# Graph attention and three message-passing layers on one core: the padded last edge group left out, the last loop body outside the loop

## The chip, the cores and the metric

The kernel runs on one core of one Trainium2 chip. The metric is the device time in microseconds (us) of a whole launch, smaller is better. A core has five engines with a program each: TensorE (PE in the profile; PEld is its weight load), VectorE (DVE), ScalarE (ACT), GpSimd (POOL) and SyncE (SP), and they meet only at semaphores.

## What is computed

A graph has 6250 nodes with 128 features and E = 200000 edges, sorted by their target `dst`. Four stages go over all edges: one attention layer (4 heads, softmax over the edges of each target), and three gated message-passing layers. Between them are dense steps over the nodes.

```python
def _L0_gnn_ref(x, edge_index, W, att):
    xh = (x @ W).reshape(-1, H, C)
    xi = xh[dst]
    xj = xh[src]
    alpha = (xi * a_i).sum(-1) + (xj * a_j).sum(-1)
    alpha = jax.nn.leaky_relu(alpha, SLOPE)
    amax = jax.ops.segment_max(alpha, dst, num_segments=N)
    ex = jnp.exp(alpha - amax[dst])
    denom = jax.ops.segment_sum(ex, dst, num_segments=N)
    alpha = ex / (denom[dst] + 1e-16)
    out = jax.ops.segment_sum(xj * alpha[..., None], dst, num_segments=N)
...
for l in range(L):                       # L = 3
    h = emb                              # for l > 0: normalised over the nodes
    e = jnp.concatenate([h[dst], h[src]], axis=1)
    hk = jax.nn.relu(e @ linA_w[l].T + linA_b[l])
    w = jax.nn.sigmoid(hk @ linB_w[l].T + linB_b[l])
    prop = jax.ops.segment_sum(w * h[src], dst, num_segments=N)
    emb = jax.nn.relu(jnp.concatenate([h, prop], axis=1) @ lin_w[l].T + lin_b[l])
...
x = _layernorm(x + _L0_gnn_ref(x, edge_index, L0_gnn_W, L0_gnn_att), axis=-1)
x = _layernorm(x + _L1_gnn_ref(x, edge_index, ...), axis=-1)
```

## The kernel before

**Groups.** Edges are worked off in groups of GE = 512 (128 partitions x 4 columns; edge 4p + t of a group stands in partition p, column t). The lists of edges are laid out in QP = 98 rows of CQ = 4 groups, so NG = QP * CQ = 392 groups are run (lines 103 to 105). 200000 edges are 390 full groups and 320 edges: group 390 (the 391st) is 5/8 full, and group 391 (the 392nd) holds no edge at all. Both lists are filled with padding first (lines 932 and 933): `dstI` with 16 * N, which matches no node, and `srcI` with 0. A padded place therefore gathers row 0 of the table like any other place would gather its own row, and its contribution is zero. In group 390 the padded places are columns 0 to 3 of partitions 80 to 127, 48 of the 128 rows of each of its four gathers; in group 391 they are all 128 of each.

**An edge stage.** GpSimd's program (from line 653) gathers the source rows: `gather` (from line 665) waits until the group's slot in the ring `G` of U = 8 slots is free (line 668, not in the first turn) and until ScalarE has copied the group's indices (line 669), and issues four indirect DMAs of 128 rows of 1 KB (line 672), whose ends count up `gathered[u]`. SyncE fetches, per four groups, the targets' offsets inside a window of 32 nodes, and per group the window's rows. Then, in the message-passing stages:

- VectorE `mp_selT` (line 1411) makes a selection matrix, TensorE `mp_hk` (line 1717) spreads the window's target terms with it, VectorE `mp_hidden` (line 1426) adds the gathered source terms: it is the first to need the gather. `mp_logit` (line 1437) does the relu and the dot product, ScalarE `gate_of` (line 876) the sigmoid, VectorE `mp_C` (line 1446) the weighted selection, TensorE `mp_agg` (line 1727) the sum over edges, VectorE `mp_E` (line 1457) adds it to the accumulator.
- In the attention stage TensorE `gat_sjT` (line 1587) is the first to need the gather; the chain goes on over `gat_e8` (lines 1599, 1603), `gat_den` (1614), `gat_nd` (1622, 1625) and VectorE's small steps up to `gat_acc` (line 1217).

Each stage is a software pipeline written out by hand: `step(k0, off)` runs, for group k0 + off, the parts of this group and of groups some steps behind (the lags in `gat_order` and `mp_order`), in this order for VectorE in a message-passing stage:

```python
mp_order = ((1, mp_hidden), (4, mp_E), (0, mp_selT), (1, mp_logit), (2, mp_C), (0, mp_sel))
```

**The loop.** On every engine a stage is: the first turn of 8 groups written out (groups 0 to 7), a hardware loop `Fori(1, NG // U)` of 48 turns of 8 groups (groups 8 to 391), and a drain, `step(NG, off, new=False)`, which only finishes the lagging parts. VectorE reads the windows' bases from memory into registers at the start of each turn (`load_bases`, line 1048, 16 registers in a turn of the loop). Behind an edge stage everything waits for the accumulator: `gat["acc"]` reaches NG before the first layer norm, `mp["acc"]` reaches km + NG before ScalarE's `hT` (line 903), from which the next layer's table, and so its first gather, is made. For groups whose edges reach beyond one window there is a further block, `extra_windows`; with these inputs its body is not run in the profile.

Of the kernel before, what the change touches and what calls it, by code (L numbers as in the profile page):

```python
# [20 lines left out]
P = 128  # L21
T = 4
GE = P * T
# [68 lines left out]
def gnn_kernel(nc, x, src, dst, W0, att, linA_w, linA_b, linB_w, linB_b, lin_w, lin_b, gamma, beta, final_w, final_b,  # L92
# [12 lines left out]
    NG = QP * CQ  # L105
    assert NG % U == 0 and QP <= P and L * 4 * D + D <= U * T * 2 * D - NBLK * D
# [33 lines left out]
    with ExitStack() as ctx:  # L140
# [73 lines left out]
        def room(lo, width):  # L214
# [106 lines left out]
        gat = dict(ahead=True, rows=lambda k, off: (gathered[off % U], 8 * k + 64 * (off // U + 1)),  # L321
                              window=lambda k, off: (win_in[off % 4], 4 * k + 16 * (off // 4 + 1)),
                              offsets=lambda k, off: (offs_in[off // 4 % 2], 2 * k + 16 * (off // U + 1)), **gat_sems)
        mp = dict(ahead=True, rows=lambda k, off: (gathered[off % U], 8 * k + (8 * NG + 64 * (off // U + 1))),
                             window=lambda k, off: (win_in[off % 4], 4 * k + (4 * NG + 16 * (off // 4 + 1))),
                             offsets=lambda k, off: (offs_in[off // 4 % 2], 2 * k + (2 * NG + 16 * (off // U + 1))),
                             **mp_sems)
# [11 lines left out]
        def one_by_one(sems, w):  # L339

            return dict(ahead=False, rows=lambda k, off: (x_rows, w * 64 + 64),
                                   window=lambda k, off: (x_win, w * 32 + 32),
                                   offsets=lambda k, off: (x_win, w * 32 + 32), **sems)
# [133 lines left out]
        def _(sp):  # L477
# [82 lines left out]
            def gat_body(k0):  # L560
                starts = load_starts(k0)
                for off in range(U):
# [5 lines left out]
            with sp.Fori(1, NG // U) as turn:  # L568
                gat_body(turn * U)
            with extra_windows(sp, 0) as at:  # L570
# [18 lines left out]
            sp.wait_ge(gat["acc"], NG)  # L589
# [3 lines left out]
            for l in range(L):  # L593
                kl = l * NG
# [28 lines left out]
                def body(k0):  # L623
                    starts = load_starts(k0)
                    for off in range(U):
# [5 lines left out]
                with sp.Fori(1, NG // U) as turn:  # L631
                    body(turn * U)
                with extra_windows(sp, l + 1) as at:
# [20 lines left out]
        def _(pool):  # L654
# [34 lines left out]
            with pool.Fori(1, NG // U) as turn:  # L689
                k0 = turn * U  # L690
                for off in range(U):
                    gather(T0, TW, k0, off, k0, (gat["R"], k0 + (off - U + 1)))
            with extra_windows(pool, 0) as at:
# [11 lines left out]
            for l in range(L):  # L705
                kl = l * NG
# [4 lines left out]
                with pool.Fori(1, NG // U) as turn:  # L711
# [8 lines left out]
        def _(act):  # L720
# [66 lines left out]
            def gat_step(k0, off, new=True):  # L787
                if new:
                    if reached(k0, off, U - LOOKAHEAD):
                        idx_slot_past(k0, off, 8 * k0)  # L790
                    copy_idx(k0, off + LOOKAHEAD)
                    gat_pen(k0, off)
                if reached(k0, off, 2) and (new or off < 2):
                    gat_exp(k0, off - 2)
                if reached(k0, off, 3):
# [4 lines left out]
            with act.Fori(1, NG // U) as turn:  # L800
# [3 lines left out]
            for off in range(3):  # L804
                gat_step(NG, off, new=False)
# [5 lines left out]
            with extra_windows(act, 0) as at:  # L811
                copy_idx_extra(at)
                for stage in (gat_pen, gat_exp, gat_den4):
                    stage(NG + at.n, 0, one_by_one(gat_sems, at.w))
# [23 lines left out]
            act.wait_ge(gat["acc"], NG)  # L838
            node_steps(act, NT // 2, ((0, ln_block), (7, ln_sqrt), (10, ln_to_x1), (10, ln_to_h)), BL)

            for l in range(L):
                kl = l * NG
                km = kl + windows_before(act, l)

                def idx_ahead(k0, off):
                    idx_slot_past(k0, off, 8 * kl + 8 * k0 + 8 * NG)
                    copy_idx(k0, off + LOOKAHEAD)

                for off in range(U - LOOKAHEAD):
                    idx_ahead(0, off)  # L850
# [28 lines left out]
                def step(k0, off, new=True):  # L879
                    if reached(k0, off, U - LOOKAHEAD) and new:  # L880
                        idx_ahead(k0, off)
                    if reached(k0, off, 1):
# [4 lines left out]
                with act.Fori(1, NG // U) as turn:  # L887
# [3 lines left out]
                step(NG, 0, new=False)  # L891

                with extra_windows(act, l + 1) as at:
                    copy_idx_extra(at)
                    gate_of(NG + at.n, 0, one_by_one(mp_sems, at.w))


                act.wait_ge(mp["acc"], km + NG)
# [31 lines left out]
        def _(dve):  # L930
# [133 lines left out]
            def gat_selT(k0, off, done=gat):  # L1064
# [3 lines left out]
                dve.wait_ge(*done["offsets"](k0, off))  # L1068
# [20 lines left out]
            def gat_mxs(k0, off, done=gat):  # L1089
                m, w = mx[:, off % 4, :], off % 4  # L1090
                dve.wait_ge(*done["window"](k0, off))
# [133 lines left out]
            def gat_step(k0, off, new=True):  # L1225
                for lag, stage in gat_order:
                    if reached(k0, off, lag) and (new or off < lag):
# [8 lines left out]
            with dve.Fori(1, NG // U) as turn:  # L1236
# [4 lines left out]
            load_bases(NG, -U, 0)  # L1241
            for off in range(5):
                gat_step(NG, off, new=False)
# [17 lines left out]
            dve.wait_ge(gat["acc"], NG)  # L1261
# [22 lines left out]
            with extra_windows(dve, 0) as at:  # L1284
                now, k0 = one_by_one(gat_sems, at.w), NG + at.n
                dve.wait_ge(x_free, at.w + (at.q + 1))
                base[0] = at.node
                make_extra_sel(at, selT16, P, pF[:, 1:2], now["selT"], now["sel"], now["window"](0, 0))
# [66 lines left out]
            for l in range(L):  # L1355
                kl = l * NG
# [50 lines left out]
                def mp_selT(k0, off, done=mp):  # L1407
                    if reached(k0, off, 4, done):
                        dve.wait_ge(done["hk"], km + k0 + (off - 3))
                    dve.wait_ge(*done["offsets"](kl + k0, off))  # L1410
# [10 lines left out]
                def mp_hidden(k0, off, done=mp):  # L1421
                    dve.wait_ge(*done["rows"](kl + k0, off))
# [38 lines left out]
                def step(k0, off, new=True):  # L1461
                    for lag, stage in mp_order:
                        if reached(k0, off, lag) and (new or off < lag):
# [7 lines left out]
                with dve.Fori(1, NG // U) as turn:  # L1471
# [4 lines left out]
                load_bases(NG, -U, 0)  # L1476
                for off in range(4):
                    step(NG, off, new=False)

                dve.wait_ge(mp["acc"], km + NG)  # L1480
                dve.sem_inc(x_free, 1)
                with extra_windows(dve, l + 1) as at:
                    now, k0 = one_by_one(mp_sems, at.w), NG + at.n
                    dve.wait_ge(x_free, at.w + (at.q + 1))
                    base[0] = at.node
                    make_extra_sel(at, selT16, S * W, pF[0:S * W, 5:6], now["selT"], now["sel"], now["window"](0, 0))
# [53 lines left out]
        def _(pe):  # L1540
# [40 lines left out]
            def gat_sjT(k0, off, done=gat):  # L1581
# [3 lines left out]
                pe.wait_ge(*done["rows"](k0, off))  # L1585
# [43 lines left out]
            def gat_step(k0, off, new=True):  # L1629
                if new:  # L1630
                    gat_sjT(k0, off)
                for lag, stage in ((3, gat_den), (4, gat_nd), (1, gat_e8)):
                    if reached(k0, off, lag) and (new or off < lag):
# [4 lines left out]
            with pe.Fori(1, NG // U) as turn:  # L1638
# [3 lines left out]
            for off in range(4):  # L1642
# [147 lines left out]
```

## Time and profile before

| | |
|---|---|
| time of the runs, median of 3 | 8248.64 us (8248.41 to 8270.31) |
| the profiled execution's own time | 8252.02 us |
| its span in the profile | 8250.5 us |
| POOL busy | 5982.9 us (73%) |
| DVE busy | 4942.3 us (60%) |
| PE busy | 4840.5 us (59%) |
| ACT busy | 1354.9 us (16%) |
| indirect DMAs issued by POOL | 6272 (1568 per stage) |
| granted TensorE clock, mean | 0.514 |

How to read it: the span runs from the first to the last instruction of the profiled execution; the 1.5 us between it and that execution's time are start and end around it. "Issue" in a chain or behind a wait is time in which the engine waited for nothing that the profile shows. A DMA's entry in the chain runs from its issue to its landing. An engine's idle time costs something only where the end of a stage waits for it.

### The profile page before, as it was taken

The numbers are of one execution on the slowest core, as the hardware profiler recorded it, in microseconds if no ns is written. First come the engines' busy times: TensorE is split into PE (matmuls) and PEld (weight loads), VectorE is DVE, ScalarE is ACT, GpSimd is POOL, SyncE is SP. The second block draws the span as 40 slices with busy tenths as digits, with TensorE's granted clock in tenths as the row PEclk, the third lists the DMA queues.
The fourth block names the chain that finished last, engine by engine and source line by source line (L and its number), as shares of the span: only waits on it lengthen the run. The fifth ranks groups of instructions, "written<-read, shape, count | busy, mean of one in ns | idle before, by whom it ended". The sixth has DMA issues, their size and how long they took to land.

```text
span 8250.5 us, 135185 instructions
## 1 busy us (share of the span) xinstructions
PE 4840.5 (59%) x26722; PEld 4122.7 (50%) x26723; DVE 4942.3 (60%) x26175; ACT 1354.9 (16%) x5278; POOL 5982.9 (73%) x6332
## 2 busy tenths in 40 slices
PE   5888888888744544454464444444546444544555
PEld 4777777777644444444444444444445444444444
DVE  7777777778755555555555555555555555555555
ACT  2333333333400000000020000000011000000002
POOL 4777777777477777777757777777766777777775
PEclk6555555555655555555565555555556555555555
DMA  4444444444444444444454444444445444444443
GB/s 135 131 131 133 131 131 131 133 132 131 127 129 131 129 129 129 130 129 130 129 152 130 129 129 131 129 129 131 129 115 166 129 130 130 129 130 130 129 129 102
DMA packets 615022, 1076.11 MB, mean 130 GB/s; under 512 B 307424, under 2 KB 372864, under 8 KB 614436
## 3 DMA queue, kind: packets, MB, share of 16 engines
q0 software_dynamic: 301056, 822.48, 35.6%
q1 hardware_dynamic: 307316, 247.87, 10.1%
q10 hardware_dynamic: 6356, 3.20, 0.2%
q14 instruction: 276, 2.26, 0.1%
q8 instruction: 18, 0.29, 0.0%
HBM read 1027.54 MB, written 45.47 MB: 130 GB/s over the span
## 4 chain that ended last, share of the span: by engine, by line
POOL 46%; issue 22%; PE 12%; DMA 9%; DVE 8%; DVEq 2%; POOLq 1%; ACT 1%; SPq 0%; ACTq 0%
POOL G L672 46%; DMA G<-mp_rows,idx 5%; DMA G<-gat_rows,idx 4%; PE ps L1727 3%; PE ps L1625 3%; DVE junk L1437 2%; PE ps L1587 2%; PE ps L1622 1%; PE ps L1614 1%; DVEq L1048 1%; PE ps L1679 0%; PE ps L1680 0%; DVE weighted L1196 0%; DVE selw L1446 0%; POOLq L669 0%
## 5 line engine op out<-in xcount | busy, mean ns | idle before, releaser
L672 POOL DMA_INDIRECT G<-mp_rows,idx x4704 | 4450.6, 946 | 1571.6 <-issue 1374.0
L1727 PE MATMUL ps<-selw,G 128*128 128x32 f32 x9408 | 2222.3, 400 | 595.8 <-DVE selw L1446 595.2
L1727 PEld LDWEIGHTS ps<-selw,G 128*128 128x128 f32 x9408 | 2094.0, 328 | 878.2 <-issue 759.3
L1426 DVE TENSOR_TENSOR pen<-ps,G 128x512 f32<-128x512 f32 x1176 | 812.9, 691 | 2740.2 <-DMA G<-mp_rows,idx 2736.3
L1717 PE MATMUL ps<-awin,ring 96*128 96x128 bf16 x4704 | 715.0, 307 | 2326.5 <-DVE ring L1411 2324.0
L672 POOL DMA_INDIRECT G<-gat_rows,idx x1568 | 1492.6, 952 | 519.8 <-issue 483.8
L1717 PEld LDWEIGHTS ps<-awin,ring 96*128 96x128 bf16 x4704 | 411.8, 132 | 2476.1 <-DVE ring L1411 2473.3
L876 ACT ACTIVATE gate<-logit,params 128x4 f32<-128x4 f32 x1176 | 349.5, 297 | 5340.9 <-DVE junk L1437 5291.5
L1437 DVE SCALAR_TENSOR_TENSOR junk<-pen,ps 128x128 f32<-128x128 f32 x4704 | 1060.4, 278 | 0.1
L1411 DVE TENSOR_TENSOR ring<-ring,ps 96x512 bf16<-96x512 bf16 x1176 | 795.6, 676 | 38.5 <-DMA ring<-rel_dst 38.5
L1625 PE MATMUL ps<-sel,weighted 128*128 128x32 f32 x3136 | 750.8, 404 | 0.0
L1625 PEld LDWEIGHTS ps<-sel,weighted 128*128 128x128 f32 x3136 | 698.0, 327 | 25.3
L1587 PE MATMUL ps<-ident,G 128*128 128x128 f32 x1568 | 428.5, 429 | 228.3 <-DMA G<-gat_rows,idx 225.8
L762 ACT ACTIVATE pen<-ring,negbig 128x512 f32<-128x512 bf16 x392 | 282.8, 722 | 1182.2 <-DVE ring L1060 1179.9
L1587 PEld LDWEIGHTS ps<-ident,G 128*128 128x128 f32 x1568 | 280.7, 217 | 251.2 <-issue 121.1
L1086 DVE CUSTOM_DVE_ANT_0 junk<-ps,pen 128x512 f32<-128x512 f32 x392 | 267.4, 682 | 217.8 <-issue 149.7
L1437 DVE DVE_READ_ACCUMULATOR junk<-pen,ps 128x1 f32 x4704 | 370.4, 79 | 0.0
L1416 DVE TENSOR_TENSOR ps<-ps,rel_all 128x128 f32<-128x128 f32 x1176 | 335.2, 285 | 0.0
L1446 DVE TENSOR_TENSOR selw<-ps,gate 128x128 f32<-128x128 f32 x1176 | 331.7, 282 | 0.2
L1614 PE MATMUL ps<-sel,ex 128*4 128x32 f32 x3136 | 231.0, 238 | 122.4 <-DVE tt L1211 122.4
L750 ACT COPY idx<-idx_all 128x4 int32 (+1 forms) x1572 | 284.0, 181 | 31.0 <-issue 24.8
L1614 PEld LDWEIGHTS ps<-sel,ex 128*4 128x4 f32 x3136 | 162.1, 105 | 253.4 <-issue 201.1
(200 smaller groups left out, 4748.8 us busy)
## 6 DMA issues: line engine op xcount, KB each, us to landing
ring<-rel_dst SPq DMA_DIRECT2D x294, 384.0 KB
G<-mp_rows,idx POOLq DMA_INDIRECT x4704
ring<-rel_dst SPq DMA_DIRECT2D x98, 512.0 KB
awin<-mp_dst_rows SPq DMA_DIRECT2D x1176, 24.0 KB
G<-gat_rows,idx POOLq DMA_INDIRECT x1568
mp_rows<-acc SPq DMA_DIRECT2D x36, 512.0 KB, 3.0
mp_dst_rows<-acc SPq DMA_DIRECT2D x36, 384.0 KB, 5.4
gat_rows<-ring SPq DMA_DIRECT2D x50, 128.0 KB, 1.9
```

The lines of the kernel that those rows point to most:

```text
L672: pool.indirect_dma_start(out=G[:, u, width * t:width * (t + 1)], out_offset=None, in_=table, in_offset=bass.IndirectOffsetOnAxis(ap=idx[: ...
L876: nc.scalar.activation(gate[:, off % 4, :], logit[:, off % 4, :], ACT.Sigmoid, bias=params[:, l, C_BB:C_BB + 1]).then_inc(done["gate"], 1)
L1411: v.tensor_tensor(selT16[0:S * W, off % 4, :], relbc16[0:S * W, off % U, :], nodeP[0:S * W, :].to_broadcast([S * W, GE]), ALU.is_equal).th ...
L1416: v.tensor_tensor(selP[:, off % 4, :].rearrange("p (t n) -> p t n", t=T), iotaP.unsqueeze(1).to_broadcast([P, T, W]), rel4, ALU.is_equal). ...
L1426: v.tensor_tensor(pen[:, off % 2, :].rearrange("p (t c) -> p t c", t=T), PS[off % 2][:, :].rearrange("p (t c) -> p t c", t=T), Grows[:, of ...
L1437: v.scalar_tensor_tensor(junk[:, P * t:P * t + P], pen[:, off % 2, P * t:P * t + P], 0.0, wP, ALU.max, ALU.mult, accum_out=logit[:, off % ...
L1446: v.tensor_tensor(selw[:, off % 4, :].rearrange("p (t n) -> p t n", t=T), one.rearrange("p (t n) -> p t n", t=T), gate[:, off % 4, :].unsq ...
L1587: i = tr(PS[off % 2][:, P * t:P * t + P], Grows[:, off % U, t, D:2 * D], ident[:, :])
L1614: i = mm(PS[4 + b][0:H, 2 * W:3 * W], ex4[:, b, H * t:H * t + H], sel[:, off % U, W * t:W * t + W], start=(t == 0), stop=(t == T - 1))
L1625: i = mm(PS[4 + b][:, 0:W], R[:, b, D * t:D * t + D], sel[:, off % U, W * t:W * t + W], start=(t == 0), stop=(t == T - 1))
L1717: i = mm(PS[off % 2][:, D * t:D * t + D], selT16[0:S * W, off % 4, P * t:P * t + P], awin[:, off % 4, :], start=True, stop=True)
L1727: i = mm(PS[2 + off % 2][:, 0:W], Grows[:, off % U, t, 0:D], selw[:, off % 4, W * t:W * t + W], start=(t == 0), stop=(t == T - 1))
```

## The change

Every stage runs GR = 391 groups. The loop runs 47 turns (groups 8 to 383) instead of 48; the last body, now with groups 384 to 390, is written out behind it together with the drain (`step(LAST, off, REST)`, LAST = 384, REST = 7). A part of a step is left out where its group would be 391. Waits that counted to 392 per stage count to 391, and those that count the landings of a ring slot take into account that slot 7 (and window slot 3) lands once less per stage. ScalarE's copies of indices, which run four groups ahead, skip group 391 but still make the first four of the next stage. The change core; the same replacement of the loop's bounds stands on all five engines:

```diff
     NG = QP * CQ
+    GR = -(-E // GE)
+    LAST = NG - U
+    REST = GR - LAST
+    assert REST == U - 1
...
+        def rows_landed(stage, k0, off):
+
+            whole = 64 * (NG // U - (off % U == U - 1))
+            return gathered[off % U], 8 * k0 + (stage * whole + 64 * (off // U + 1))
...
-                kl = l * NG
+                kl = l * GR
                 km = kl + windows_before(pool, l)
                 pool.wait_ge(t1_out, 16 * NQ * (l + 1))
                 for off in range(U):
-                    gather(T1, TW, 0, off, kl + NG, None)
-                with pool.Fori(1, NG // U) as turn:
+                    gather(T1, TW, 0, off, kl + GR, None)
+                with pool.Fori(1, NG // U - 1) as turn:
                     k0 = turn * U
                     for off in range(U):
-                        gather(T1, TW, k0, off, kl + k0 + NG, (mp["agg"], km + k0 + (off - U + 1)))
+                        gather(T1, TW, k0, off, kl + k0 + GR, (mp["agg"], km + k0 + (off - U + 1)))
+                for off in range(REST):
+                    gather(T1, TW, LAST, off, kl + (LAST + GR), (mp["agg"], km + (LAST + off - U + 1)))
...
-            def idx_slot_past(k0, off, before):
-
-                act.wait_ge(gathered[(off + LOOKAHEAD) % U], before + 64 * ((off + LOOKAHEAD) // U))
...
+            def idx_ahead(stage, k0, off, stop):
+
+                if off < U and (off + LOOKAHEAD < stop or off + LOOKAHEAD >= U):
+                    if stage > 0 or reached(k0, off, U - LOOKAHEAD):
+                        act.wait_ge(*rows_landed(stage, k0, off + LOOKAHEAD - U))
                     copy_idx(k0, off + LOOKAHEAD)
...
-                def step(k0, off, new=True):
+                def step(k0, off, stop=U):
                     for lag, stage in mp_order:
-                        if reached(k0, off, lag) and (new or off < lag):
+                        if reached(k0, off, lag) and off - lag < stop:
                             stage(k0, off - lag)
...
-                with dve.Fori(1, NG // U) as turn:
+                with dve.Fori(1, NG // U - 1) as turn:
                     k0 = turn * U
                     load_bases(k0, -U, U)
                     for off in range(U):
                         step(k0, off)
-                load_bases(NG, -U, 0)
-                for off in range(4):
-                    step(NG, off, new=False)
-
-                dve.wait_ge(mp["acc"], km + NG)
+                load_bases(LAST, -U, U)
+                for off in range(REST + 4):
+                    step(LAST, off, REST)
+
+                dve.wait_ge(mp["acc"], km + GR)
```

What stands on GpSimd in the first message-passing stage, before: the loop's last group, its end, and then at once the loads of the block of further windows (line 452).

```order
114 L672 DMA G<-mp_rows,idx 128x256 x4
115 L669 REGISTER_ALU
116 L672 DMA G<-mp_rows,idx 128x256 x4
117 L711 REGISTER_ALU
118 L711 COMPARE_AND_BRANCH
119 L452 TENSOR_LOAD windows
```

And in the change, the same place; of the seven groups of four gathers behind the loop's branch the first and the last two stand here.

```order
117 L687 DMA G<-mp_rows,idx 128x256 x4
118 L728 REGISTER_ALU
119 L728 COMPARE_AND_BRANCH
120 L683 REGISTER_ALU
121 L687 DMA G<-mp_rows,idx 128x256 x4
```

```order
130 L683 REGISTER_ALU
131 L687 DMA G<-mp_rows,idx 128x256 x4
132 L683 REGISTER_ALU
133 L687 DMA G<-mp_rows,idx 128x256 x4
134 L465 TENSOR_LOAD windows
```

The program is 28 gathers longer there, and everything behind it in GpSimd's program stands at another place in memory than before; up to the first stage's loop nothing on any engine has moved but the numbers in the instructions.

VectorE's end of the same stage in the change: the last step with a new group, then the drain.

```order
1337 L1433 TENSOR_TENSOR ps<-ps,rel_all 128x128
1338 L1442 REGISTER_ALU
1339 L1443 TENSOR_TENSOR pen<-ps,G 128x512
1340 L1474 ISA
1341 L1474 TENSOR_TENSOR acc<-acc,ps 128x32
1342 L1454 SCALAR_TENSOR_TENSOR junk,logit<-pen,ps 128x128 x4
1343 L1463 TENSOR_TENSOR selw<-ps,gate 128x128
1344 L1474 ISA
1345 L1474 TENSOR_TENSOR acc<-acc,ps 128x32
1346 L1463 TENSOR_TENSOR selw<-ps,gate 128x128
1347 L1474 ISA
1348 L1474 TENSOR_TENSOR acc<-acc,ps 128x32
```

The hidden layer's step (`mp_hidden`, line 1443 in the change, 1426 before) at number 1339 is that of group 390; behind it stands what stood behind group 391's before, without a `mp_selT` between.

## Rows read from the trace of the kernel before

**Rows 1.** The page: busy time, and the chain that ended last by engine and line.

```profile
PE 4840.5 (59%) x26722; PEld 4122.7 (50%) x26723; DVE 4942.3 (60%) x26175; ACT 1354.9 (16%) x5278; POOL 5982.9 (73%) x6332
...
POOL 46%; issue 22%; PE 12%; DMA 9%; DVE 8%; DVEq 2%; POOLq 1%; ACT 1%; SPq 0%; ACTq 0%
```

**Rows 2.** Timeline: start, duration, engine, line, instruction, idle before; first message-passing stage, POOL.

```profile
2195.81 0.96 POOL L672 DMA_INDIRECT G<-mp_rows,idx  x1 [34.75 <-DMA mp_rows<-acc]
...
4150.56 0.95 POOL L672 DMA_INDIRECT G<-mp_rows,idx  x1 [0.30 <-issue]
4151.81 0.95 POOL L672 DMA_INDIRECT G<-mp_rows,idx  x1 [0.30 <-issue]
...
4155.56 0.95 POOL L672 DMA_INDIRECT G<-mp_rows,idx  x1 [0.30 <-issue]
```

**Rows 3.** Timeline, all engines, end of the first message-passing stage (groups 389, 390, 391).

```profile
4148.39 0.69 DVE L1426 TENSOR_TENSOR pen<-ps,G 128x512 f32<-128x512 f32 x1 [2.38 <-DMA G<-mp_rows,idx]
...
4153.50 0.69 DVE L1426 TENSOR_TENSOR pen<-ps,G 128x512 f32<-128x512 f32 x1 [2.49 <-DMA G<-mp_rows,idx]
...
4160.61 0.69 DVE L1426 TENSOR_TENSOR pen<-ps,G 128x512 f32<-128x512 f32 x1 [4.49 <-DMA G<-mp_rows,idx]
...
4162.61 3.62 PE L1727 MATMUL ps<-selw,G 128*128 128x32 f32 x16 [4.73 <-DVE selw L1446]
...
4166.37 0.19 DVE L1457 TENSOR_TENSOR acc<-acc,ps 128x32 f32 x1 [1.52 <-PE ps L1727]
```

**Rows 4.** Busy time by stretch, same place: last columns PEclk, DMA share, GB/s.

```profile
4145.00:4150.00 5.00, 2.49 (x14) 2.12 (x13) 2.62 (x14) 0.38 (x2) 3.78 (x5) 0.50 0.36 102
...
4157.50:4160.00 2.50, 0.39 (x2) 0.25 (x2) 0.00 (x0) 0.00 (x0) 0.00 (x0) 0.50 0.80 72
4160.00:4162.50 2.50, 0.00 (x0) 0.00 (x0) 1.85 (x12) 0.11 (x1) 0.00 (x0) 0.50 0.00 0
```

**Rows 5.** Timeline, VectorE, ends of the second and the third message-passing stage.

```profile
6165.89 0.69 DVE L1426 TENSOR_TENSOR pen<-ps,G 128x512 f32<-128x512 f32 x1 [2.42 <-DMA G<-mp_rows,idx]
...
6173.12 0.69 DVE L1426 TENSOR_TENSOR pen<-ps,G 128x512 f32<-128x512 f32 x1 [4.61 <-DMA G<-mp_rows,idx]
...
8180.28 0.69 DVE L1426 TENSOR_TENSOR pen<-ps,G 128x512 f32<-128x512 f32 x1 [2.45 <-DMA G<-mp_rows,idx]
...
8188.22 0.69 DVE L1426 TENSOR_TENSOR pen<-ps,G 128x512 f32<-128x512 f32 x1 [5.32 <-DMA G<-mp_rows,idx]
```

**Rows 6.** The chain in order of time, third message-passing stage: start, us, what.

```profile
8182.33 5.29 DMA G<-mp_rows,idx
...
8187.73 0.04 DVEq L1425
8187.77 0.45 issue
```

**Rows 7.** Timeline, TensorE, end of the attention stage (groups 388, 390, 391).

```profile
2061.67 1.09 PE L1587 MATMUL ps<-ident,G 128*128 128x128 f32 x4 [0.54 <-DMA G<-gat_rows,idx]
...
2071.82 1.09 PE L1587 MATMUL ps<-ident,G 128*128 128x128 f32 x4 [0.95 <-DMA G<-gat_rows,idx]
2078.57 1.09 PE L1587 MATMUL ps<-ident,G 128*128 128x128 f32 x4 [2.55 <-DMA G<-gat_rows,idx]
```

**Rows 8.** Who waited for whom, 2230 to 4155 us: total us, times, longest us.

```profile
POOL G L672 <- issue: 442.0, 1451, 0.3
POOL G L672 <- PE ps L1727: 15.5, 51, 0.3
```

**Rows 9.** The chain, attention stage: VectorE at the start of a turn.

```profile
1999.15 2.34 issue
2001.61 1.11 DVEq L1048
```

**Rows 10.** Timeline, VectorE, start of the last turn of the attention stage's loop.

```profile
2043.66 0.69 DVE L1086 CUSTOM_DVE_ANT_0 junk<-ps,pen 128x512 f32<-128x512 f32 x1 [4.21 <-issue]
```

**Rows 11.** Timeline, VectorE, the final layer norm's loop of ten blocks a turn.

```profile
8226.42 0.16 DVE L1532 SCALAR_TENSOR_TENSOR bnm<-bmv,brs 128x1 f32<-128x1 f32 x1 [0.24 <-issue]
...
8235.34 0.16 DVE L1532 SCALAR_TENSOR_TENSOR bnm<-bmv,brs 128x1 f32<-128x1 f32 x1 [0.24 <-issue]
```

More of the change, by code:

```diff
@@ L567, in _ @@
             gat_body(0)
-            with sp.Fori(1, NG // U) as turn:
+            with sp.Fori(1, NG // U - 1) as turn:
                 gat_body(turn * U)
+            gat_body(LAST, REST)
             with extra_windows(sp, 0) as at:
@@ L799, in _ @@
                 gat_step(0, off)
-            with act.Fori(1, NG // U) as turn:
+            with act.Fori(1, NG // U - 1) as turn:
                 k0 = turn * U
@@ L803, in _ @@
                     gat_step(k0, off)
-            for off in range(3):
-                gat_step(NG, off, new=False)
+            for off in range(REST + 3):
+                gat_step(LAST, off, REST)
             def copy_idx_extra(at):
@@ L886, in _ @@
                     step(0, off)
-                with act.Fori(1, NG // U) as turn:
+                with act.Fori(1, NG // U - 1) as turn:
                     k0 = turn * U
@@ L890, in _ @@
                         step(k0, off)
[L891 removed]
+                for off in range(REST + 1):
+                    step(LAST, off, REST)
                 with extra_windows(act, l + 1) as at:
                     copy_idx_extra(at)
[L895 to L898 removed]
+                    gate_of(GR + at.n, 0, one_by_one(mp_sems, at.w))
+                act.wait_ge(mp["acc"], km + GR)
                 act.sem_inc(waited, 1)
@@ L1240, in _ @@
                     gat_step(k0, off)
-            load_bases(NG, -U, 0)
-            for off in range(5):
-                gat_step(NG, off, new=False)
+            load_bases(LAST, -U, U)
+            for off in range(REST + 5):
+                gat_step(LAST, off, REST)
             def make_extra_sel(at, tile, rows, node, selT_done, sel_done, window):
@@ L1470, in _ @@
                     step(0, off)
-                with dve.Fori(1, NG // U) as turn:
+                with dve.Fori(1, NG // U - 1) as turn:
                     k0 = turn * U
@@ L1627, in gat_nd, with gat_step @@
                 i.then_inc(done["nd"], 1)
[L1629 to L1633, printed above, removed]
+            def gat_step(k0, off, stop=U):
+                for lag, stage in ((0, gat_sjT), (3, gat_den), (4, gat_nd), (1, gat_e8)):
+                    if reached(k0, off, lag) and off - lag < stop:
                         stage(k0, off - lag)
@@ L1637, in _ @@
                 gat_step(0, off)
-            with pe.Fori(1, NG // U) as turn:
+            with pe.Fori(1, NG // U - 1) as turn:
                 k0 = turn * U
@@ L1641, in _ @@
                     gat_step(k0, off)
-            for off in range(4):
-                gat_step(NG, off, new=False)
+            for off in range(REST + 4):
+                gat_step(LAST, off, REST)
             with extra_windows(pe, 0) as at:
                 for stage in (gat_sjT, gat_e8, gat_den, gat_nd):
-                    stage(NG + at.n, 0, one_by_one(gat_sems, at.w))
+                    stage(GR + at.n, 0, one_by_one(gat_sems, at.w))
             def ln_turn(turn, off):
@@ L1738, in _ @@
                     step(0, off)
-                with pe.Fori(1, NG // U) as turn:
+                with pe.Fori(1, NG // U - 1) as turn:
                     k0 = turn * U
@@ L1742, in _ @@
                         step(k0, off)
-                for off in range(3):
-                    step(NG, off, new=False)
+                for off in range(REST + 3):
+                    step(LAST, off, REST)
                 with extra_windows(pe, l + 1) as at:
                     for stage in (mp_hk, mp_agg):
-                        stage(NG + at.n, 0, one_by_one(mp_sems, at.w))
+                        stage(GR + at.n, 0, one_by_one(mp_sems, at.w))
             def f_linear(turn, off):
```

108 lines of the change are left out of this document (54 added, 54 removed).

## Prediction

> **What bounds the kernel now.** I read the page first, then GpSimd's timeline inside a stage and at its end, then all engines at the four stage ends. No engine is full: GpSimd is busy 73% of the span, yet the chain that ended last is GpSimd and its "issue" to 68% [rows 1]. The timeline tells why: a gather takes 0.95 us and the next one starts 0.30 us later, always, so 1.25 us apart. From the first gather of the first message-passing stage at 2195.81 to its 1568th at 4155.56 are 1567 steps of 1.2506 us [rows 2]. What GpSimd has to issue sets the time inside a stage: four gathers, 5.00 us a group. The other engines wait in each group (VectorE 2.38 us before group 389's hidden layer, [rows 3]).
>
> At the end of a stage another thing counts. The last gather of group 390 is issued at 4150.56 [rows 2] and the step that needs it starts at 4153.50 [rows 3], 2.94 us later. The last of group 391 is issued at 4155.56 and its step starts at 4160.61, 5.05 us later: this landing is 2.11 us late. Group 391 is all padding, its 512 places all gather row 0. While they are under way the DMA engines are 0.80 busy and move 72 GB/s, where they were 0.36 busy at 102 GB/s before, and after the landing they are idle [rows 4]: 0.80/72 against 0.36/102 is 3.1 times the DMA time per byte. A gather is 128 KB (131072 bytes), which at 72 GB/s is 1.8 us, longer than the 1.25 us between issues, so the four queue up: 4 x 1.8 = 7.3 us from about 4153 ends at 4160.4. So I read the late landing as the price of 128 reads of one address, that is, of the padding, and not of standing last.
>
> **The change, part by part.**
>
> *One group less, message-passing stages.* The chain goes gather, hidden layer, logit, gate, weighted selection, sum, accumulator, and then the relu for all nodes. Behind the hidden layer of the stage's last group the drain has the same instructions before and after, in the same order (the last excerpt of the order shows it), and the engines are idle when it starts. So the end moves by the distance between the starts of the last two hidden layers: 4160.61 - 4153.50 = 7.11 us in the first stage [rows 3]; 6173.12 - 6165.89 = 7.23 and 8188.22 - 8180.28 = 7.94 in the other two [rows 5]. In each 5.00 are the four gathers not issued, and the rest is lateness. The third has more because its landing took 5.29 us and VectorE then spent 0.45 us on "issue" between wait and work [rows 6], against 4.85 us, and nothing of the kind, in the first.
>
> *The attention stage.* Here TensorE's transposes need the gather first: 2078.57 for group 391, 2071.82 for group 390 [rows 7], 6.75 us apart. The drain behind is again the same; it is longer, but it is a chain of its own length and starts 6.75 us earlier.
>
> *Sum of the gains:* 7.11 + 7.23 + 7.94 + 6.75 = 29.0 us.
>
> *Leaving the loop earlier.* All engines leave the loop seven groups before the end and go on in straight code; a loop was left once per stage before too, but GpSimd had nothing to issue behind it. Only a pause on GpSimd would count in full. From below it is nothing: GpSimd's gaps stay at 0.3 us at the longest, over the whole loop with its 48 branches back [rows 8], and the first turn is straight code of the same kind. From above take the longest pause of the sort in the trace, VectorE's 2.34 us of "issue" at the start of a turn of the attention loop [rows 9], four times 9.4 us. I take the lower end, being GpSimd's own rows, with 0.1 us a stage for unevenness: 0.5 us, rounded up. The Trainium skill (Runtime: NRT & Kernel Launch, "Instruction fetch mechanics") says that instructions are fetched ahead in blocks strictly in sequence, and that only a taken branch out of the two blocks held stalls. Leaving a loop takes no branch, so by that rule the term is 0 and the gain 29.0. By the upper end of the rows the gain would be 19.6.
>
> *The other engines' exits.* VectorE needs 2.34 us and then 1.11 us for the register load at a turn's start [rows 9]. In the attention stage it stands 4.21 us before group 384's step [rows 10], yet at group 388 TensorE waits for the gather again (0.54 us, [rows 7]): caught up in four groups. The new tail has seven. In the message-passing stages a group leaves 2.4 us free [rows 3], so such a pause is gone a group or two later. Cost 0, hidden under GpSimd's issues; if that cover were gone, up to 4.2 us in one stage.
>
> *Padding that stays.* Group 390 has 48 padded rows of 128 in each gather. Its landing (2.94 us) is 0.11 us behind that of group 389 (4148.39 - 4145.56 = 2.83, the issue being four steps of 1.25 before the 4150.56 of [rows 2]). This is in the distances above already. *Registers, waits with other counts, the index copies four groups ahead:* the same number of instructions for each group that is left, and ScalarE is 16% busy [rows 1]: 0.
>
> Net: 29.0 - 0.5 = 28.5 us. The profiled execution took 8252.0 us (its span 8250.5 and 1.5 around it), so the sum gives 8223.5 for such a one; the median of the runs shown is 3.4 lower, 8248.6, and from there it gives 8220.1. I predict **8220**.
>
> **The rivals.**
>
> *B, the last gather lands late whatever it reads.* Then group 390's last landing would take 5 us too, and only the four issues are saved: 4 x 5.00 = 20.0 us, 8228.6. For it: all the late ones seen stand last. Against it: the DMA engines were busy at a low rate [rows 4], not idle.
>
> *C, GpSimd pauses where it leaves the loop*, 2.34 us at most in each stage [rows 9]: gain 19.1 to 28.5 us, 8220 to 8229.5. For it: VectorE has such pauses. Against: GpSimd has none [rows 8].
>
> *D, slower: the moved loops.* GpSimd's program grows by 28 gathers per stage, so the three message-passing loops stand elsewhere in memory. If a loop there fits the fetch less well, each of its turns pauses: 3 x 47 = 141 turns. At 28.5/141 = 0.20 us a turn the gain is gone, at (28.5 + 24.7)/141 = 0.38 us the kernel is measurably slower. The final layer norm's loop on VectorE shows 0.24 us once per turn, 8.9 us apart [rows 11]: that price gives 34 us, and 8254; 2.34 us a turn would give 8550. Against it: GpSimd's loop of the first message-passing stage, already at another place than the attention stage's, shows no pause at all [rows 8]. The same section of the Trainium skill (Runtime: NRT & Kernel Launch, "Instruction fetch mechanics") speaks for this case: a branch back to a block no longer held stalls. By that rule it would decide whether GpSimd's loop spans more than two blocks, which no run here shows.
>
> *That the change doesn't drop the group* is ruled out by the order of instructions: 28 gathers stand behind the loop, not 32.
>
> **How the numbers follow.** About 0.3% (24.7 us) is what a measurement of this kernel can tell from no change. My forecast 0.67, B 0.12, C 0.16, D 0.05. The forecast lies only 3.8 us beyond that bound, and the runs before spread over 22 us, so 0.07 of its 0.67 may come out as no change; B falls wholly in there, C nearly so (0.02 beyond), and D for 0.02, with 0.03 slower. Faster 0.62, same 0.35, slower 0.03. The range: if every stage gained the third's 7.94 us the sum would be 31.8 and the time 8217, less a little, 8216; at the other end B and C end at 8229, and a median like the profiled execution is 3.4 higher: 8233.
>
> **What would show it.** Right: 1564 gathers per stage, 1.25 us apart through the loop's end; the last hidden layer of each message-passing stage about 2.9 us behind the last issue, with 4.6 to 5.3 us of VectorE's idle time before it gone to 2.5; no stretch with the DMA engines at 0.8 and 72 GB/s; each stage 6.7 to 7.9 us shorter, nothing changed between the stages. Wrong: a last landing of 5 us (B); a gap over 0.3 us on GpSimd 28 gathers before a stage's end (C), or once per 32 gathers in the loop (D).

## The result, and the profile after

The changed kernel took 8217.6 us (median of 7 runs, 8216.4 to 8238.9), the kernel before on the same chip 8248.1 (7 runs, 8246.5 to 8270.3): 30.5 us less, ratio 0.9965 with a 95% interval of 0.9956 to 0.9975, which is a gain of 21 to 36 us. Predicted were 8220 us and a gain of 28.5.

The profiled execution of the change is its slowest: 8238.9 us (span 8237.1), the first of its seven; the first of before was 22 us above its median too. So its rows carry about 21 us that the median does not have, and the first rows show where they lie. The page, busy time, the chain and GpSimd's two groups:

```profile
PE 4828.4 (59%) x26657; PEld 4110.2 (50%) x26658; DVE 4929.9 (60%) x26111; ACT 1352.1 (16%) x5266; POOL 5983.1 (73%) x6316
...
POOL 46%; issue 22%; PE 11%; DMA 9%; DVE 8%; DVEq 2%; POOLq 1%; ACT 1%; SPq 0%; ACTq 0%
...
L687 POOL DMA_INDIRECT G<-mp_rows,idx x4692 | 4450.8, 949 | 1564.2 <-issue 1383.9
...
L687 POOL DMA_INDIRECT G<-gat_rows,idx x1564 | 1492.4, 954 | 519.5 <-issue 483.5
```

Against [rows 1] there are 16 gathers fewer, and GpSimd is busy for the same time: one takes 949 ns where the execution before had 946. The timeline of GpSimd over the first message-passing stage shows it as a spacing, the counterpart of [rows 2]:

```profile
2192.37 0.97 POOL L687 DMA_INDIRECT G<-mp_rows,idx  x1 [34.08 <-DMA mp_rows<-acc]
...
4116.68 0.95 POOL L687 DMA_INDIRECT G<-mp_rows,idx  x1 [0.30 <-issue]
4117.94 0.95 POOL L687 DMA_INDIRECT G<-mp_rows,idx  x1 [0.30 <-issue]
...
4151.80 0.95 POOL L687 DMA_INDIRECT G<-mp_rows,idx  x1 [0.30 <-issue]
4202.91 0.95 POOL L687 DMA_INDIRECT G<-mp_rows,idx  x1 [50.16 <-DMA mp_rows<-acc]
```

1563 steps between 2192.37 and 4151.80 are 1.2536 us each, against 1.2506 before. Over the four stages the wider spacing comes to 16.5 us (20.0 - 3.47 of the table below), most of the excess of this execution. Twenty-eight gathers before the end, at 4116.68 to 4117.94, GpSimd leaves the loop, and the gap is the usual 0.30 us. In all four stages of the change no gap between two gathers is above 0.32 us.

The end of the same stage, all engines, then VectorE in the second and third stage and TensorE in the attention stage, against [rows 3, 5, 7]:

```profile
4149.65 0.69 DVE L1443 TENSOR_TENSOR pen<-ps,G 128x512 f32<-128x512 f32 x1 [2.44 <-DMA G<-mp_rows,idx]
...
4154.86 0.69 DVE L1443 TENSOR_TENSOR pen<-ps,G 128x512 f32<-128x512 f32 x1 [2.59 <-DMA G<-mp_rows,idx]
...
4160.69 0.19 DVE L1474 TENSOR_TENSOR acc<-acc,ps 128x32 f32 x1 [1.52 <-PE ps L1742]
...
6164.87 0.69 DVE L1443 TENSOR_TENSOR pen<-ps,G 128x512 f32<-128x512 f32 x1 [2.58 <-DMA G<-mp_rows,idx]
...
8175.25 0.69 DVE L1443 TENSOR_TENSOR pen<-ps,G 128x512 f32<-128x512 f32 x1 [2.50 <-DMA G<-mp_rows,idx]
...
2076.12 1.09 PE L1604 MATMUL ps<-ident,G 128*128 128x128 f32 x4 [0.90 <-DMA G<-gat_rows,idx]
```

VectorE's idle time before a stage's last hidden layer was 4.49, 4.61 and 5.32 us and is 2.59, 2.58 and 2.50. The last step starts 3.06 us behind the last issue (4154.86 against 4151.80), where it was 5.05. Busy time by stretch, against [rows 4] (last columns DMA share and GB/s):

```profile
4149.00:4154.00 5.00, 2.44 (x13) 2.13 (x12) 2.62 (x13) 0.38 (x2) 2.85 (x3) 0.50 0.35 103
4154.00:4156.50 2.50, 0.10 (x1) 0.00 (x0) 1.60 (x9) 0.00 (x0) 0.00 (x0) 0.50 0.02 7
```

The stretch with the DMA engines at 0.80 and 72 GB/s is gone; they keep their usual share (0.35 at 103 GB/s) nearly to the last landing.

The span closes to the hundredth when it is cut at the gathers. T is a stage's time from its first to its last gather, D the time from there to the next stage's first gather, in the last row to the end of the span.

| us | T before | T after | D before | D after |
|---|---|---|---|---|
| attention | 1968.96 | 1967.85 | 122.05 | 119.26 |
| message passing 1 | 1959.75 | 1959.43 | 52.46 | 51.11 |
| message passing 2 | 1959.94 | 1958.92 | 54.14 | 51.31 |
| message passing 3 | 1960.23 | 1959.21 | 68.17 | 64.75 |

With the first gather 0.46 us later (105.26 against 104.80) that is 3.47 + 10.39 - 0.46 = 13.4 us, as the two spans say. The 3.47 are 4 x 5.0 us not issued, less what the wider spacing gave back in this execution; the 10.39 stand at the stages' ends. With before's spacing the sum is 20.0 + 10.4 - 0.5 = 29.9, beside the 30.5 of the medians.

### The profile page after: what moved, and what is told of

Its sections match the earlier page's. It is cut to its first block, busy times and chain, and to the rows that moved or that the text cites. A ratio compares the mean times of both kernels' runs of the same rounds, so it can differ in the third digit from the quotient of the medians.

```text
span 8237.1 us, 134783 instructions
## 1 busy us (share of the span) xinstructions
PE 4828.4 (59%) x26657; PEld 4110.2 (50%) x26658; DVE 4929.9 (60%) x26111; ACT 1352.1 (16%) x5266; POOL 5983.1 (73%) x6316
## 4 chain that ended last, share of the span: by engine, by line
POOL 46%; issue 22%; PE 11%; DMA 9%; DVE 8%; DVEq 2%; POOLq 1%; ACT 1%; SPq 0%; ACTq 0%
POOL G L687 46%; DMA G<-mp_rows,idx 5%; PE ps L1742 3%; DMA G<-gat_rows,idx 3%; PE ps L1642 3%; DVE junk L1454 2%; PE ps L1604 1%; PE ps L1639 1%; PE ps L1631 1%; DVEq L1065 1%; PE ps L1694 0%; PE ps L1695 0%; DVE selw L1463 0%; DVE sel L1073 0%; POOLq L684 0%
```

## The experiments

The theory (A): the padded group is late because each of its gathers reads one row 128 times. The main rival (B): it is late because it is last. Also open was what the peeling costs by itself.

The runs came on four chips, and these differ. On three of them the kernel before took 10448 to 10453 us, on the fourth 8249 us, as in the first measurement. Each result stands beside runs of before on its own chip.

### Padding spread, and the change taken apart

The first edit, on the kernel before, fills the 704 padded places (192 in group 390, 512 in group 391; the third series' expectation says 576, which is wrong) with real row numbers:

```diff
+            sp.dma_start(srcI[QF:QF + 1, E - QF * QW:QW],
+                         src[0:QW - (E - QF * QW)].rearrange("(q e) -> q e", q=1)).then_inc(edges_loaded, 16)
...
-            dve.wait_ge(edges_loaded, 96)
+            dve.wait_ge(edges_loaded, 112)
```

> The kernel before, all 392 groups and loops, but the 704 padded places of src hold the sources of the first 704 edges instead of 0, so that group 391 reads 512 different rows. Theory A (the last landing is late because 128 descriptors read one row): group 391's step starts about 2.9 us behind its last issue, as group 389's did, and the four lateness terms go, 2.11 + 2.23 + 2.94 + 1.75 = 9.0 us: 8239 us against 8248. Rival B (the last gather is late whatever it reads): no change, 8248 us, and 5 us from last issue to step.

The second is the change with the same edit.

> The changed kernel with the padded places of group 390 spread over different rows in the same way. Theory A: group 390's landing was only 0.1 us late, so at most 0.5 us over four stages, not to be told from the change. Rival B: the same, 0. A gain of over 3 us would mean that 48 padded rows of 128 cost more at a stage's end than I read.

The third is the change with eight groups in the last body, 392 in all, so that of the change only the peeling is left, with its rewritten waits and index copies:

```diff
-    GR = -(-E // GE)
+    GR = NG
...
-            whole = 64 * (NG // U - (off % U == U - 1))
+            whole = 64 * (NG // U)
...
-            whole = 16 * (NG // 4 - (off % 4 == 3))
+            whole = 16 * (NG // 4)
```

> The changed kernel's code, but with 392 groups: the loop runs 47 turns and the last eight groups stand outside. The code moved as in the change, nothing is left out. My sum (pauses at the loop's exit 0.5 us in all, moved loops 0): 8248 to 8249 us, and GpSimd's gaps 0.30 us at 32 gathers before a stage's end. Rival C (a pause of up to 2.34 us per stage on GpSimd): up to 8257. Rival D (moved loops pause each turn): 8282 or more.

The fourth is the first with group 203, far from any end, reading row 0 only:

```diff
+            then(v.memset(idx_all[:, 203 * T:204 * T], 0))
```

> The padding spread as in the first, and the indices of group 203 (in the middle of each stage) all set to 0, so that its gathers read one row: this group's sources are wrong for the output. Theory A: group 203's step starts about 2 us late, 5 us behind its last issue, with the DMA engines near 0.8 busy at some 72 GB/s, and group 204 about on time or little late; the stage's end isn't later, since GpSimd goes on at 1.25 us, and no late landing at its end. Rival B: nothing late in the middle, and group 391's landing 5 us.

These four ran on a chip where before takes 10452.7 us. A second series has the change itself in place of the second kernel, and its chip was of the same sort:

> The kernel before with its padded places reading different rows, once more, since the first four kernels ran on a chip where the kernel before took 10453 us and GpSimd waited for landings inside the stages: there a stage's end says little. Where the kernel before takes 8248: theory A 8239 us (ratio 0.9989) and the last landing of each stage 2.9 us behind its issue; rival B 8248 us and 5 us. Where it takes 10450 again, neither shows in the time, as before.

> The change itself beside the others on one chip. At 8248 for the kernel before: 8217 to 8221 us, as first measured. On a chip like the last, where the stages are bound by landings of 5.4 to 7.6 us a group: 391 of 392 groups, a gain of 5.4 x 3 + 7.6 = 24 us or a little more, about 10428 of 10452.

> 392 groups, 47 turns and eight groups outside the loop. On the last chip this read 1.0013 (1.0004 to 1.0022), 13 us slower, where the runs of the kernel before spread over 32 us. At 8248 for the kernel before: my theory 8248 to 8249 us, rival C up to 8257, rival D 8282 or more. If the 13 us come again, the code's new place costs something that the first comparison of the change hid.

> Padding spread, and group 203's indices all 0, so that group reads one row in the middle of each stage (its sources are wrong for the output). Theory A: step of group 203 about 5 us behind its last issue, neighbours 2.9 us, the DMA engines near 0.8 busy at 72 GB/s for some 2 us, the last landing of the stage 2.9 us. Rival B: group 203 as its neighbours, last landing 5 us.

| | median us | before us | ratio (95%) |
|---|---|---|---|
| spread, first series | 10447.0 | 10452.7 | 0.9998 (0.9989 to 1.0007) |
| change and spread | 10435.5 | 10452.7 | 0.9990 (0.9981 to 0.9999) |
| peeling alone, first series | 10465.7 | 10452.7 | 1.0013 (1.0004 to 1.0022) |
| group 203, first series | 10450.4 | 10452.7 | one run |
| spread, second series | 10451.1 | 10450.5 | 1.0002 (0.9992 to 1.0011) |
| the change itself | 10434.4 | 10450.5 | 0.9984 (0.9975 to 0.9993) |
| peeling alone, second series | 10460.4 | 10450.5 | 1.0011 (1.0002 to 1.0020) |
| group 203, second series | 10457.0 | 10450.5 | one run |

What these chips do differently the profile of the spread kernel shows (second series). First its page, then VectorE in the middle of the first message-passing stage, then two stretches there:

```profile
another core or an unknown queue 45%; DVE 24%; issue 17%; PE 10%; DVEq 4%; ACT 0%; DMA 0%; SPq 0%; POOL 0%; ACTq 0%; POOLq 0%
...
L1428 DVE TENSOR_TENSOR pen<-ps,G 128x512 f32<-128x512 f32 x1176 | 806.7, 686 | 3860.3 <-remote 3709.2
```

```profile
4006.48 0.69 DVE L1428 TENSOR_TENSOR pen<-ps,G 128x512 f32<-128x512 f32 x1 [8.67 <-remote]
...
4009.01 0.68 DVE L1428 TENSOR_TENSOR pen<-ps,G 128x512 f32<-128x512 f32 x1
...
4011.53 0.68 DVE L1428 TENSOR_TENSOR pen<-ps,G 128x512 f32<-128x512 f32 x1
...
4024.89 0.69 DVE L1428 TENSOR_TENSOR pen<-ps,G 128x512 f32<-128x512 f32 x1 [10.75 <-remote]
```

```profile
4002.50:4005.00 2.50, 0.00 (x0) 0.00 (x0) 0.00 (x0) 0.00 (x0) 1.35 (x2) 0.50 0.35 103
4005.00:4007.50 2.50, 0.00 (x0) 0.00 (x0) 1.02 (x3) 0.00 (x0) 0.26 (x1) 0.50 0.10 36
```

GpSimd's issues no longer head the chain. VectorE waits (8.67 and 10.75 us here) for something the profile has no name for, ahead of the step that needs the gather, then works off groups 2.52 us apart. In the wait the DMA engines fall to 0.10, so bandwidth is not what is short. Nor do the gathers keep the engines longer: the page gives their queue 27.5% of 10452.7 us, 0.46 us a gather, against 35.6% of 8250.5 us and 0.47 us before. A message-passing group takes 2336.8 us / 391.75 = 5.96 us here (T of the first such stage) instead of 5.00, an attention group 3015.8 / 391.75 = 7.70. What holds the landings back no run here tells.

What follows from the two series. *Padding, by the clock: undecided.* At the end of the first message-passing stage of the spread kernel (second series) VectorE still has five groups to work off: their hidden layers start 2.70 to 12.81 us behind the last issue, 2.52 us apart. Behind such a backlog a last landing that is 2 us late moves nothing, so A and B forecast the same, and neither the spread padding nor group 203 moved the time. *Peeling alone costs* 13.0 and 9.8 us by the medians. *The group left out gains* what one group takes in each stage: from peeling alone to the change, on one chip, 10460.4 - 10434.4 = 26.0 us, beside 3 x 5.96 + 7.70 = 25.6. The whole change is 16.1 us faster there, and its interval still excludes 1. The change with spread padding, 17.2 us faster by the medians on another chip, is not to be told from the change: spreading the 48 padded rows left in each gather of group 390 shows no gain here.

*Padding, by the trace: one row is slow to read there too.* The first message-passing stage's end, peeling alone (padding as in before) and then the spread kernel, second series:

```profile
5585.00:5587.50 2.50, 0.61 (x4) 0.34 (x4) 2.33 (x12) 0.09 (x1) 0.12 (x1) 0.50 0.83 80
```

```profile
5587.50:5590.00 2.50, 1.98 (x11) 1.75 (x9) 0.87 (x8) 0.38 (x2) 0.95 (x1) 0.50 0.38 105
5590.00:5592.50 2.50, 0.81 (x5) 0.41 (x5) 2.30 (x12) 0.05 (x1) 0.00 (x0) 0.50 0.04 10
```

With the same group at the same place, the last gathers ran at 0.83 and 80 GB/s when they read one row and at 0.38 and 105 GB/s when they read many. And in the middle of a stage, behind the one-row gathers of group 203, which GpSimd issued at 6865.01 to 6868.76 in the second message-passing stage (first series):

```profile
6862.50:6865.00 2.50, 0.06 (x1) 0.06 (x1) 0.00 (x0) 0.49 (x2) 1.89 (x2) 0.50 0.36 105
...
6867.50:6870.00 2.50, 0.00 (x0) 0.00 (x0) 0.00 (x0) 0.00 (x0) 1.89 (x2) 0.50 0.70 89
6870.00:6872.50 2.50, 0.00 (x0) 0.00 (x0) 0.41 (x1) 0.00 (x0) 0.00 (x0) 0.50 0.72 77
```

In the second series a stretch behind group 203's gathers has 0.66 at 77 GB/s in the same stage. The high share goes with the row, not with the end. That speaks against B, but in a share, not yet in microseconds; how late group 203's own step was can't be read under VectorE's backlog.

### Every gather from one row, or from the same 128 rows

To get the price into the time whatever the chip, it was made large in two more kernels. The first is before with this, ahead of the first gather:

```diff
+            then(v.memset(idx_all[:, :], 0))
```

> The kernel before with the whole table of gather indices set to 0, so all 6272 gathers read row 0 128 times, as the padded group's do; the sums over edges are therefore of row 0 alone, all else runs as before. Theory A (descriptors that read one and the same row cost the DMA engines about three times as much per byte, and that is why the padded group lands late): the DMA engines' share rises from about 0.36 at 102 GB/s to 0.75 or more at 70 to 90 GB/s all through the edge stages. At the 0.80 and 72 GB/s of rows 4, a gather of 128 KB fills the engines for 1.46 us, more than the 1.25 us in which GpSimd issues one: on the chip of the first profile the time would be 9000 us or more, on the slower chip of the last runs at least what it is. Rival B (the last group is late because it is the last, whatever it reads): share 0.36, and the time of before within 0.3%.

The second repeats column 0 of the index table in all columns:

```diff
+            then(v.tensor_copy(idx_all[:, 1:], idx_all[:, 0:1].to_broadcast([P, (NG + LOOKAHEAD) * T - 1])))
```

> The kernel before with every column of the table of gather indices set to column 0, so all 6272 gathers read the same 128 scattered rows, one each per partition; the sums over edges are of those rows alone, all else runs as before. Theory A (it is one and the same row within a gather that costs): share about 0.36 at about 102 GB/s wherever GpSimd is not waiting, and the time of before within 0.3%. Rival C (it is a small stretch of memory read over and over, not one row, that costs): share clearly above 0.36 at the same GB/s, and the time between that of before and that of the run with one row.

This chip was like the first: before took 8249.4 us. One row: **11629.5 us**. The same 128 rows: **8249.8 us**. (One run each; the first is off by 3380 us, for the second the rows below count, not the clock.) The stretch from 4000 to 5000 us for one row, from 3000 to 4000 for the same 128 rows and for before:

```profile
4000.00:5000.00 1000.00, 352.16 (x1693) 299.58 (x1692) 369.45 (x1836) 55.55 (x282) 532.93 (x564) 0.50 1.00 91
```

```profile
3000.00:4000.00 1000.00, 498.40 (x2399) 424.44 (x2398) 523.88 (x2600) 78.66 (x399) 756.37 (x800) 0.50 0.45 129
```

```profile
3000.00:4000.00 1000.00, 498.87 (x2400) 424.86 (x2400) 524.00 (x2600) 78.89 (x400) 756.29 (x801) 0.50 0.46 130
```

With one row the DMA engines are full, and 564 gathers take 1000 us: one every 1.77 us. The other transfers have their share in that. The gathers' own queue stands on the two pages, one row first, then before:

```profile
q0 software_dynamic: 301056, 822.48, 86.4%
```

```profile
q0 software_dynamic: 301056, 822.48, 35.6%
```

86.4% of 11627.9 us over 6272 gathers is 1.60 us of all the engines for each, against 0.47 us: 3.4 times as much for the same bytes. Reading the same 128 rows 6272 times costs nothing. So it is the same row within a gather that costs, not a small set of rows read over and over (rival C of that expectation falls, for scattered rows; 128 neighbouring rows were not tried).

The second kernel also decides A against B on the fast sort of chip, since its padded group reads 128 rows like all others, and it leaves the loops as before does. VectorE and GpSimd at the end of the first message-passing stage:

```profile
4159.80 0.94 POOL L672 DMA_INDIRECT G<-mp_rows,idx  x1 [0.30 <-issue]
4210.13 0.94 POOL L672 DMA_INDIRECT G<-mp_rows,idx  x1 [49.39 <-DMA mp_rows<-acc]
```

```profile
4162.89 0.69 DVE L1427 TENSOR_TENSOR pen<-ps,G 128x512 f32<-128x512 f32 x1 [2.59 <-DMA G<-mp_rows,idx]
```

It is still group 391 and still last, and its step starts 3.09 us behind the last issue instead of 5.05. In the order of the stages (attention first):

| last step behind last issue, us | before | same 128 rows | the change |
|---|---|---|---|
| attention | 4.81 | 2.90 | 3.01 |
| message passing 1 | 5.05 | 3.09 | 3.06 |
| message passing 2 | 5.16 | 2.95 | 3.04 |
| message passing 3 | 5.89 | 3.34 | 2.90 |
| sum | 20.91 | 12.28 | 12.01 |

A stands: 8.6 us of lateness go when the group stays and only its rows change, 8.9 us when it is left out. B, by which the last group would stay at 5 us, falls. The whole run was no faster all the same: its first gather came 3.41 us later (108.21 against 104.80), and its four stages took 1.89, 1.63, 1.30 and 0.51 us longer from first to last gather, GpSimd's spacing being up to 0.0012 us wider. That is 8.7 us lost, and 11.0 us gained in the times between the stages; the spans differ by 2.3 (8248.2 against 8250.5).

### Spread padding and peeling alone, once more

The last two were meant to time both kernels on the faster sort, and ran on a third chip of the slower sort:

> The kernel before with the 576 padded edge places filled with real row numbers (from a second load of the start of the sources), still 392 groups, nothing left out of the loops. If this lands on a chip where before takes about 8249 us, theory A (the padded group is late because it reads one row) takes off the four lateness terms alone, 2.11 + 2.23 + 2.94 + 1.75 = 9.0 us: about 8240 us; rival B (late because it is last) leaves 8249 us, within 1 us. On the slower chips both leave it unchanged, as in the first two series.

> The change with its last body given all eight groups (392 groups issued, the last one padded), so only the peeling is left of it. On a chip where before takes about 8249 us: the theory that the other engines' loop exits lie under GpSimd's issues gives 8249 us, within 1 us (0.5 us more at most); the rival that the exits cost there what they cost on the slower chips gives 8259 to 8262 us. On a slower chip again 0.11 to 0.13% more.

Before took 10448.4 us here. Spread padding: 10455.2, ratio 1.0003 (0.9994 to 1.0012). Peeling alone: 10457.8, ratio 1.0009 (1.0000 to 1.0019). So on the three chips of that sort the peeling has cost 13.0, 9.8 and 9.4 us. Neither kernel ever ran where before takes 8249 us, and their time there is not measured.

## Why the prediction was right

**What bounds the kernel: right.** GpSimd's steps set the time inside a stage in the change too, and only a stage's end has another price.

**Four gathers a stage, 20.0 us: right.** 1564 are left, with 0.30 us between them, and in the median nothing else fits. In the profiled execution this term is hidden under its wider spacing: only 3.5 us of it are seen there. The two profiled executions alone would have misled by 17 us.

**Lateness of the padded group, 9.0 us: right in kind and size, though one step of its working was lucky.** The four terms were 1.75, 2.11, 2.23 and 2.94 and came out as 1.80, 1.99, 2.12 and 2.99. The reason given (reads of one address, not the last place) is now shown, by the kernel with the same 128 rows. The working that gave "4 x 1.8 = 7.3 us from about 4153 ends at 4160.4" agreed with the step at 4160.61 by luck. Before, two stretches cut where the engines' work begins and ends:

```profile
4153.50:4159.50 6.00, 2.52 (x12) 2.13 (x12) 2.62 (x13) 0.30 (x1) 2.40 (x3) 0.50 0.70 87
4159.50:4160.50 1.00, 0.00 (x0) 0.00 (x0) 0.00 (x0) 0.00 (x0) 0.00 (x0) 0.50 0.01 0
```

The 72 GB/s were the mean of a stretch whose last half microsecond was idle. The four gathers (6.00 us at 87 GB/s are their 4 x 131 KB) took 1.5 us each and were through at 4159.5; the step came 1.1 us later, where in the changed kernel at most 0.5 us lie between (engines idle from about 4154.4, step at 4154.86). Behind the last issue the engines were through 3.9 us later before and 2.6 in the change, so about 1.3 of the 2.0 us of lateness are transfer time; what makes up the rest is not shown. The 1.77 us between gathers of the one-row kernel are no test of the 1.8 either, as they hold other transfers; the gather's own price there was 1.60 us of all the engines. At this stage's end it was less, 0.70 of 6.00 us for four, 1.05 us each; why repetition raises it is open.

**Leaving the loop, 0.5 us: not to be told from 0.** Rival C expected a pause on GpSimd of up to 2.34 us in each stage. Who waited for whom in the changed kernel, 2230 to 4150 us, against [rows 8]:

```profile
POOL G L687 <- issue: 451.9, 1482, 0.3
POOL G L687 <- PE ps L1742: 13.7, 45, 0.3
POOL G L687 <- ACT idx L769: 1.8, 6, 0.3
```

No wait above 0.3 us, in the loop or at its exit, and none above 0.32 us between gathers in the other stages: C and D (a pause in each turn of the moved loops) both fall. The times between the stages fell by 10.4 us in the change and by 11.0 in the kernel with the same 128 rows, which is not peeled; of that 8.9 and 8.6 us are lateness. The other 1.5 and 2.4 us lie behind the last steps, where the prediction had no change; single ends there moved by +0.6 to -1.4 us between these executions. What the peeling cost at the ends, if anything, is within that.

**The other engines' exits, 0 because hidden: right, and the cover matters.** At VectorE's exit from the attention loop the pause of [rows 10] did not come again; it shrank from 4.21 to 1.25 us:

```profile
2045.11 0.69 DVE L1103 CUSTOM_DVE_ANT_0 junk<-ps,pen 128x512 f32<-128x512 f32 x1 [1.25 <-issue]
```

The Trainium skill (Runtime: NRT & Kernel Launch, "Instruction fetch mechanics") says that a taken branch whose target is outside the fetched blocks stalls, and that for code in sequence the cost of crossing into a new block is mostly hidden. These two rows agree with it: the place of the pause is the same, the branch back is gone. In the kernel with the same 128 rows, which keeps the branch, the pause there is 4.20 us. A gain there is worth nothing on the chips where GpSimd's issues hide VectorE. On the others, where they do not, I expected up to 4.2 us in one stage if the cover were gone; peeling measured 9 to 13 us over all four, more than that aside allowed. In the traces the attention stage is not longer with it (3012.1 to 3020.8 us against 3011.0 to 3020.8), and the message-passing stages scatter by 5 us and more among kernels with the same loops, so where those 9 to 13 us lie stays open.

**The median.** 28.5 us were predicted and 30.5 measured; the interval of 21 to 36 holds both. Rival B's 20.0 lies just below that interval, and the stage ends exclude it more firmly than the clock does.

## What to carry to other kernels

When a gather bounds a stage, look at what its padding reads: 128 reads of one row took 1.60 us of all DMA engines for 128 KB, 128 different rows 0.47 us, well within GpSimd's 1.25 us between issues. Padding that can't be left out is cheaper with spread, harmless rows, where its landing is waited for: here at a stage's end, 2 us each time. A padded group in the middle of a stage was tried only on the slower sort of chip, where it didn't show in the time. Leaving work out gained about that work's time on both sorts of chip, on the slower one counted from the peeled kernel. The peeling cost 9 to 13 us on the slower sort and nothing that the ends show on the other, where it was not timed alone.

## What the runs showed of the hardware that was not expected

- Chips fell into two sorts for this kernel: 8248 to 8249 us, and 10448 to 10453 us on three others. On the latter VectorE has waits such as 8.67 and 10.75 us before the step that needs a gather, with the DMA engines at 0.10 in part of the wait; GpSimd's issues stay 0.95 us long and 1.25 us apart where it issues.
- Gathers of the same 128 rows over and over are neither faster nor slower than gathers of scattered ones (0.45 and 129 GB/s against 0.46 and 130), but 128 reads of one row fill the DMA engines (1.00 at 91 GB/s), 1.60 us of them a gather against 0.47.
- GpSimd's spacing varied between executions, 1.2506 us in one and 1.2536 in another; over the four stages that was 16.5 us, more than half of the effect that was measured.
